# Joining and spreading the experts' token lists at other points of the schedule, in a fused cross attention and mixture-of-experts kernel

## The reference

```python
x = x + xattn(latents=..., context=ctx_768, mask)       # 8 batches x 512 tokens x 256
# feed-forward, experts choose tokens: 4096 tokens, 16 experts, 256 tokens each
logits = xn @ router_weight.T + router_bias
_, idx = top_k(logits.T, 256)                           # each expert's 256 tokens
xe = xn[idx]
h = gelu(einsum('ecd,efd->ecf', xe, fc1_weight) + fc1_bias)
y = einsum('ecf,edf->ecd', h, fc2_weight) + fc2_bias
output = zeros.at[idx].add(y * gates)                   # then divided by the token's sum of gates
```

## Time and profile before

| | |
|---|---|
| median of 3 runs | 1190.92 us (1190.54 to 1196.23) |
| the profiled execution | 1190.16 us, span 1188.3 us |
| busy over the span | PE 1021.8 us (86%), DVE 798.6 (67%), ACT 683.9 (58%), POOL 817.0 (69%) |
| expert stage, from expert 2's start to expert 15's | 977.65 to 1165.41 us |

### The profile page before, as it was taken

One profiled execution on the slowest core, in us unless ns is written; L12 is line 12 of the kernel. 1 busy time (PEld: TensorE's weight loads), 2 busy tenths in 40 slices (PEclk: granted clock), 3 DMA queues, 4 the chain that ended last, 5 costly groups with the idle time before them and its releaser, 6 DMA issues.

```text
span 1188.3 us, 17496 instructions
## 1 busy us (share of the span) xinstructions
PE 1021.8 (86%) x6038; PEld 633.2 (53%) x6038; DVE 798.6 (67%) x1839; ACT 683.9 (58%) x1328; POOL 817.0 (69%) x891
## 2 busy tenths in 40 slices
PE   3769999999999999999999999988630398999996
PEld 2535445544644644554464464443210288899996
DVE  3676677866786876787677668683148757776752
ACT  5646656676576566567657655535224136666663
POOL 3205896797598599679759859969603158888883
PEclk9869999999999999999999999999865599999998
DMA  6010010011011001001110010010027146666652
GB/s 173 3 57 1 19 40 2 0 37 42 2 55 42 2 26 54 19 1 55 42 38 1 7 32 6 2 38 1 11 63 215 45 83 192 216 212 180 209 171 28
DMA packets 73480, 71.99 MB, mean 61 GB/s; under 512 B 38608, under 2 KB 67408, under 8 KB 69296
## 3 DMA queue, kind: packets, MB, share of 16 engines
q1 hardware_dynamic: 65392, 62.08, 16.7%
q0 software_dynamic: 6336, 8.70, 4.1%
q10 hardware_dynamic: 1664, 0.10, 0.1%
HBM read 56.97 MB, written 13.83 MB: 60 GB/s over the span
## 4 chain that ended last, share of the span: by engine, by line
PE 68%; POOL 11%; DVE 8%; issue 5%; ACT 4%; DMA 1%; ACTq 1%; POOLq 0%; DVEq 0%
PE bank L718 53%; PE pair_bank L718 10%; POOL prob_sum L1257 8%; ACT probs L1002 2%; DVE c_in L1560 2%; PE bank L791 2%; PE bank L743 2%; DVE list L1695 1%; POOL w_lo L1291 1%; DMA out_x<-y_out,token_index 1%; POOL z_lo L1236 1%; POOL out_x L1326 1%; DVE masked_scores L1477 1%; PE bank L871 1%; ACT c_in L1002 1%
## 5 line engine op out<-in xcount | busy, mean ns | idle before, releaser
L1257 POOL TENSOR_TENSOR prob_sum<-prob_sum,probs 128x256 f32<-128x256 f32 x640 | 475.4, 774 | 80.8 <-ACT probs L1002 74.3
L1002 ACT ACTIVATE probs<-bank,mask_col 128x512 f32<-128x512 f32 x256 | 161.9, 685 | 109.9 <-PE bank L718 108.1
L1477 DVE CUSTOM_DVE_ANT_0 masked_scores<-pair_bank,mask_bias 128x512 bf16<-128x512 f32 x256 | 166.3, 687 | 80.4 <-PE pair_bank L718 80.2
L718 PE MATMUL bank<-probs,v_nat 128*64 128x512 f32 x768 | 205.1, 616 | 0.4 <-ACT probs L1002 0.4
L1470 DVE TENSOR_REDUCE maxima<-pair_bank 128x2 f32<-128x1024 f32 x64 | 78.3, 1224 | 46.7 <-PE pair_bank L718 46.7
L1002 ACT ACTIVATE probs<-bank 128x512 f32<-128x512 f32 x128 | 69.5, 595 | 66.0 <-PE bank L718 65.2
L718 PE MATMUL pair_bank<-k_hi,q_hi 64*128 64x512 f32 x384 | 91.8, 472 | 14.4 <-DVE maxima L1477 7.7
L718 PE MATMUL bank<-q_hi,k_hi 64*128 64x512 f32 x384 | 94.2, 484 | 10.6 <-ACT probs L1002 8.8
L1257 POOL TENSOR_TENSOR prob_sum<-probs 128x256 f32<-128x256 f32 x64 | 44.9, 734 | 80.6 <-ACT probs L1002 68.8
L1507 DVE RECIPROCAL bank<-bank 128x128 f32<-128x128 f32 x64 | 58.5, 943 | 58.4 <-PE bank L718 58.4
L718 PEld LDWEIGHTS bank<-q_hi,k_hi 64*128 64x128 f32 x384 | 37.3, 184 | 106.4 <-ACT probs L1002 55.3
(11 more groups left out here) (235 smaller groups left out, 2584.8 us busy)
## 6 DMA issues: line engine op xcount, KB each, us to landing
w_raw<-in_fc SPq DMA_DIRECT2D x16, 1024.0 KB, 4.8
w<-in_fc SPq DMA_DIRECT2D x16, 1024.0 KB, 6.9
c_in<-in_ctx SPq DMA_DIRECT2D x16, 384.0 KB, 3.4
x_in<-in_x SPq DMA_DIRECT2D x8, 512.0 KB, 4.8
out_x<-x_in SPq DMA_DIRECT2D x8, 512.0 KB, 3.5
rows_scratch<-xr_nat SPq DMA_DIRECT2D x8, 512.0 KB, 3.6
c_in<-in_ctx SPq DMA_DIRECT2D x16, 128.0 KB, 3.5
b_rows<-in_fc_bias SPq DMA_DIRECT2D x16, 128.0 KB, 6.1
```

The costliest lines, as they stand in the source:

```text
L718: return pe.matmul(out, lhsT, rhs, start=start, stop=stop, skip_group_check=True)
L1002: return act.activation(out, a, f, bias=bias, scale=scale)
L1257: last = tt(total[:, half], first[:, half], p[:, half], ALU.add)
L1477: last = dve.tensor_tensor_reduce(masked_scores[:, hh, :], pair_bank[:, hh, :], mask_bias[:, 512 * g:512 * (g + 1)], 1.0, MASKED, ALU.add, ...
```

## The change

The join, the spread and the gather stand at other points of the list. `list_join` goes from point 18, right behind `list_count`, to point 21, behind `turn_tokens`. `list_spread` goes from point 21 of the even expert to point 4 of the following odd one, behind the `scatter` pieces of that point. The gather for the next expert goes from point 1 to point 5, in even and odd experts. Nothing is computed differently. Experts 0 and 1 keep their order, which `first_expert` writes out.

```diff
             if at == 18 and counts:
                 add("list_count", counts)
-                add("list_join", counts)
-            if at == 1 and 2 <= e < E - 1:
+            if at == 4 and e % 2 and 2 < e < E - 1:
+                add("list_spread", group_of(e + 1))
+            if at == 5 and 2 <= e < E - 1:
                 add("gather", e + 1)
             if at == 3 * FT - 4 and e + 1 < E:
                 add("turn_tokens", e + 1)
             if at == 3 * FT - 3 and counts:
-                add("list_spread", counts)
+                add("list_join", counts)
```

## The result

Over ten timed executions each, the changed kernel took 1200.07 us in the median (1197.55 to 1205.37) and the kernel before, run beside it, 1195.63 us (1190.54 to 1200.30). The ratio is 1.005, 95% interval 1.0027 to 1.0073: slower, by half a percent; the interval leaves out 1, and the prediction had called less than 0.5% (6 us) no change that can be told. The profiled execution took 1197.55 us with a span of 1195.7, against 1188.3 before, and 6.7 of those 7.4 us arose between the start of expert 2 and the start of expert 15: 1172.78 - 978.37 = 194.41 us where it was 187.75.

What follows compares the result with a forecast made beforehand. PE's chain, with the held join's stall in even experts, was taken as the bound, POOL's queue nearly as long. Experts 2 to 14 summed to 187.1 us against 187.8; with +1.4 clock and +1.5 landings, +2.2: 1193 us, range 1184 to 1203.

Steps and rivals of the forecast that it cites:

- the prediction's two signs of being wrong: PE doesn't wait at the transposes, or odd experts take 14.5 us or more.
- caught by `hot_lo`: Rival: in odd experts the first gather waits for `hot_lo` too; 6 us more, 1199 us; chance 0.18.
- The join is held by POOL, not slow: Even experts: the join waits for POOL's `w1_lo` pair, 3.07 us against 0.18; moving it takes out 2.4 us.
- The gather behind the scatters sets an expert's length: Each expert: the gather follows two scatter issues, its landing holds the transposes; PE alone would need 12.6 or 13.2 us.
- Even experts 13.93 us: Even expert's period with its gather held by `hot_ids`, second gather issued at 9.16 us; 13.3 if not held.
- Expert 2, +3.8 us: Expert 2: the gather for expert 3 goes behind its late scatters, so expert 3 starts 3.8 us later, once.
- Odd experts 13.70 us: Odd expert's period with the first gather at 7.44 us, held by `hot_hi` only; 14.9 if also by `hot_lo`.
- The gather starts inside `hot_hi`: Odd experts: the first gather comes at 7.44 us, `hot_hi` runs 6.6 to 7.75, so the gather ends at 8.63.
- price (b): POOL's issue spacing: scatter to scatter 1.93 us, scatter to what follows 1.88, gather to gather 1.29.
- Expert 14, 13.3: Expert 14: no hot operations and no join, so a period of 13.3 us.
- The one slow clock spell that I added: PE at its lower clock level once, after idling 0.6 to 1.2 us before the transposes: +1.4 us.
- The rival in which nothing takes the stall's place: The stall goes, the gather lands in time, POOL is no bound: 1175 us; chance 0.12, wholly or mostly.

Runs made afterwards that it cites:

- the join from PSUM: The kernel before, order untouched, with the join in three operations, each with one operand in PSUM: 1180.32 us, ratio 0.990.
- the last experiment: The changed kernel with `hot_lo` moved from point 9 to point 17 of odd experts: 1209.71 us, ratio 1.0135 to the kernel before.

## Why the prediction was right, and which term was off

The forecast, no change that can be told with more weight on slower than on faster, and the range of 1184 to 1203 us held, though not by much. The forecast was +0.2%, the measured ratio +0.5%. The median of 1200.07 us is 7.1 above the forecast; 4.7 of these are the kernel before itself, whose median beside it was 1195.63 us where the forecast started from 1190.92. And one of the prediction's two signs of being wrong, odd experts of 14.5 us or more, was met by three experts, 5, 7 and 9. What came is the forecast case in most experts and the rival "caught by `hot_lo`" (0.18) in those three.

- *The join is held by POOL, not slow.* Shown, by the join from PSUM: 3.06 us became 0.18 with nothing moved. PE's gain of 2.4 us in an even expert, if nothing else changes, was 1.8 there; the spread's matmul stays between the transposes and the next start, which takes 2.39 us where it takes 2.01 in an odd expert.

  A page bears on this: the Trainium skill, "SBUF — State Buffer", section "Who interferes with whom", says that a VectorE instruction with at most one SBUF input, outside the modes in which it uses both port pairs, does not contend with GpSimd, and one with two does while GpSimd reads SBUF. The runs agree, with 0.18 against 3.06 us. The page also holds, as an inference, that such a `tensor_tensor` leaves GpSimd's descriptor generation alone. Here the gathers' issues were held: in the changed kernel each first gather issued inside one ended 0.87 to 0.89 us after it. A gather also reads its row numbers, `token_index`, and no run here tells whether it is that reading or the descriptors that was held.
- *The gather behind the scatters sets an expert's length.* Shown for the changed kernel: its chain runs over the gather, and with the gather moved back in even experts alone these go from 14.1 to 13.63 us and PE no longer waits for one. Moved alone in the kernel before, the gather costs 13.6 us in the stage, but there partly by another way: a longer held join, and the lower clock behind it in odd experts.
- *Even experts 13.93 us.* They took 14.07 to 14.29. Landing was taken as 2.8 us; in expert 6 it took 2.78, from the issue at 1053.41 to 1056.19. What was too small is the last term, 1.87 us from the transposes to the next start; it is 2.07 in the changed kernel. It had been read off a piece of the chain that begins at 1063.88, but in PE's timeline of the kernel before the transposes begin earlier, 2.01 us ahead of that start:

```profile
1063.72 0.60 PE L950 MATMUL bank<-ident,gathered 128*128 128x128 f32 x4
```

- *Expert 2, +3.8 us.* It was +4.7. The gather was not late: the transposes began 19.54 us after expert 2's start, where the sum had 22.15 - 1.87 = 20.28. But behind 4.94 us in which PE stood idle its granted clock was at the lower of its two levels, and from the transposes to the next start it took 1001.38 - 997.91 = 3.47 us in place of 2.07.
- *Odd experts 13.70 us, 14.9 if the gather is caught by `hot_lo`.* Here is the term that was off. The step that failed is "The gather starts inside `hot_hi`". It held in expert 11 (13.85). In experts 5, 7 and 9 the gather came at 8.0 to 8.3 us, inside `hot_lo`, and they took 14.92 to 14.95, the rival's number. The rival had warned of a margin of only 0.3 us; what used it up was the first scatter's issue, which price (b) has as 1.62 us (1.93 from one scatter to the next) and which took 2.49. A scatter's issue of 2.49 us stood in the rows from the start, but was priced only as a delay of POOL's pair. Three such experts at 1.2 us make 3.7, expert 13, which has no hot operations but the same long issue, another 0.8.
- *Expert 14, 13.3.* It took 13.91: its second gather was issued at 8.70 us (8.55 in the sum), the transposes began 3.14 us later (2.9 in the sum), and the next start 2.07 after them.
- *The one slow clock spell that I added* came, in another place: not in an odd expert but behind the wait of expert 2. In the later experts PE waits at most 1.81 us at the transposes, and the granted clock is 1.00 over the first 3 us of each expert from 4 to 14. That the count of one came true is luck: it rested on waits of 0.6 to 1.2 us, shorter than the list stalls, but PE waited 1.76 to 1.81 us in experts 5, 7 and 9 and kept its clock, where in the kernel before 1.69 and 1.67 us came just ahead of the two slow starts. The windows of the changed kernel, with the granted clock behind the five engines' busy times:

```profile
994.00:997.80 3.80, 0.00 (x0) 0.00 (x0) 0.00 (x0) 0.00 (x0) 3.47 (x3) 0.86 0.56 108
997.80:999.00 1.20, 1.09 (x5) 1.10 (x6) 0.00 (x0) 0.00 (x0) 1.20 (x2) 0.50 0.00 0
...
1001.50:1003.00 1.50, 1.50 (x9) 1.50 (x9) 1.50 (x2) 0.10 (x1) 0.00 (x0) 0.50 1.34 393
1003.00:1005.00 2.00, 2.00 (x17) 2.00 (x16) 1.16 (x5) 1.78 (x5) 1.30 (x1) 0.86 0.78 319
```

  The level of 0.50 lasts from ahead of the transposes to past 1003, so expert 3's 13.80 us hold a part of it as well.
- *The rival in which nothing takes the stall's place* (1175 us) was out for this change. The join from PSUM, in the old order, comes near it with 1180.

In the stage the sum, without that spell and the allowance for landings, gave 187.1 us against 194.41. The 7.3 us are 3.7 + 0.8 in odd experts, 0.9 in expert 2, 0.6 in expert 14, 1.1 in the even ones from 4 to 12, and small ones in experts 3 and 11.

What makes a scatter's issue take 2.49 us stays open. The kernel before shows it too, in second scatters, and it was not free there: POOL's pair of `w1_lo`, to whose end the join is held and PE with it, started only behind it, at 1047.11. Both 1.81 and 2.49 us come with the issue starting 0.1 us after the first `h_lo`; in expert 3, where it starts 0.16 us ahead of `h_lo`, it takes 1.62. That fits a hold by `h_lo`, which reads both its operands from SBUF, but doesn't say what decides between the two lengths, and was not tried. The spread's operations aren't needed for the long one. Nor is a `w2_lo` pushed back by the join: in expert 15 no join stands ahead of it, and in expert 9 of the last experiment the join took 0.18 us. In the changed kernel with the join from PSUM the long issue occurred in none of thirteen experts, nor in any of the kernel before with the gather moved alone. From the changed kernel, VectorE and POOL in expert 15:

```profile
1173.41 1.76 DVE L1727 TENSOR_TENSOR w_lo<-w,w_hi 128x1536 fp32r<-128x1536 f32 x1 [0.68 <-ACT w_hi L1003]
```

```profile
1176.04 2.49 POOL L1327 DMA_INDIRECT out_x<-y_out,token_index  x1 [5.09 <-DVE y_out L1751]
```

## What to carry to other kernels

When an operation on a few partitions takes 3 us, look at which engine ends with it and where its operands lie before moving it: here one operand in PSUM was worth 1%, moving the operation 0.5% at best. When a step is moved in a hand-written order, write down for each queue what it is moved past: here a gather that had covered POOL's wait for VectorE went behind that wait, and the 8.6 us that the even experts gained were spent and more. A piece that has slack where it stands may have none four points later, and then its landing, its issue and everything that may hold its issue are on the path.

## What the runs showed of the hardware that was not expected

The issue of an expert's first scatter on POOL takes 1.6 to 1.8 us in most experts of these kernels and 2.4 to 2.8 in some, and the longer one shifts what follows enough to fall into another operation's hold. A gather's issue that starts inside `hot_hi` gets away between it and `hot_lo`, though they follow without a gap (it ends 0.87 us after `hot_hi`, with `hot_lo` still running), while the join, started inside the first operation of POOL's pair (3.06 us), and `hot_lo`, begun just ahead of it (5.82 us), did not get in between the pair's two. The lower clock does not follow the length of PE's wait alone: in the kernel before it came behind 1.67 and 1.69 us and not behind 2.11 (expert 4), and in the changed one it stayed away at 1.81.
